# A decoder layer on one core: a tenth weight buffer in the space of the exponents, an earlier request for the fifth expert, a new timetable of the attention steps, and another order of loads and stores at the end

## The reference

```python
# 1. a mixer with cumulative sums over the tokens (cut)
out = (bil + alpha * tri) / counts + (bias_b + alpha * bias_t);  x += out @ Wo.T
# 2. cross attention, 16 heads of 32, 750 keys
x += softmax(Q @ K.T * SCALE) @ V @ Wo.T
# 3. experts that choose tokens: E = 32 experts, K = 8 tokens each, H = 2048
probs = softmax(x @ gate_w.T + gate_b, axis=tokens)
vals, idx = top_k(probs, K)                      # per batch and expert
merged = sum_k x[idx_k] * vals_k                 # one row per batch and expert
h = gelu([merged, 1] @ w1[e]);  o = [h, 1] @ w2[e]
x[idx_k] += o * vals_k                           # scattered back
```

## Time and profile before

| | us |
|---|---|
| median of 3 runs | 2212.28 |
| lowest and highest | 2208.69, 2214.53 |
| profiled execution | 2212.52 |
| its span in the profile | 2210.8 |

### The profile page before, as it was taken

One profiled execution on the slowest core, in us unless ns is written; L12 is line 12 of the kernel. 1 busy time (PEld: TensorE's weight loads), 2 busy tenths in 40 slices (PEclk: granted clock), 3 DMA queues, 4 the chain that ended last, 5 costly groups with the idle time before them and its releaser, 6 DMA issues. The chain is left out here.

```text
span 2210.8 us, 41404 instructions
## 1 busy us (share of the span) xinstructions
PE 1842.7 (83%) x12594; PEld 1207.2 (55%) x12594; DVE 1011.4 (46%) x2542; ACT 747.3 (34%) x1551; POOL 823.9 (37%) x591
## 2 busy tenths in 40 slices
PE   7889999999999999999999999986665656655644
PEld 5667777777777776777777767753111111111111
DVE  1355757657667676676676665751100000000003
ACT  3144435435454454454444544542100000000000
POOL 0255545555555556555555565552000000000000
PEclk9799999999999999999999999988877777777776
DMA  5324333243243333332433333266999999999996
GB/s 171 84 68 101 81 91 98 76 101 82 77 105 83 88 94 83 92 85 76 109 83 84 95 85 89 70 240 233 406 422 421 423 421 420 421 422 421 420 365 238
DMA packets 142370, 421.35 MB, mean 191 GB/s; under 512 B 32140, under 2 KB 78188, under 8 KB 117756
## 3 DMA queue, kind: packets, MB, share of 16 engines
q1 hardware_dynamic: 135580, 411.70, 54.6%
q10 hardware_dynamic: 5760, 8.15, 1.0%
q0 software_dynamic: 992, 1.02, 0.1%
HBM read 307.37 MB, written 17.14 MB: 147 GB/s over the span
## 5 line engine op out<-in xcount | busy, mean ns | idle before, releaser
L1172 DVE TENSOR_REDUCE maxes<-bank 112x1 f32<-112x376 f32 (+1 forms) x1024 | 511.3, 539 | 118.5 <-PE bank L1393 114.9
L974 ACT ACTIVATE probs<-bank 125x448 f32<-125x448 f32 x768 | 400.0, 547 | 140.5 <-PE bank L1415 139.5
L1809 PE MATMUL bank<-ring,hid_T 128*32 128x512 f32 x1024 | 177.9, 858 | 201.3 <-DMA ring<-in_L_ffn_w 196.4
L848 POOL TENSOR_TENSOR psum_keys<-psum_keys,probs 125x896 f32<-125x896 f32 x127 | 266.7, 2100 | 211.9 <-ACT probs L974 202.5
L1415 PE MATMUL bank<-q_st,k_st 98*125 98x224 f32 x1536 | 334.6, 304 | 8.5 <-DMA q_st<-max_two 5.6
L1393 PE MATMUL bank<-k_st,q_st 96*112 96x376 f32 (+1 forms) x1024 | 318.9, 357 | 21.3 <-DVE maxes L1172 18.1
L1415 PEld LDWEIGHTS bank<-q_st,k_st 98*125 98x125 f32 x1536 | 256.8, 190 | 61.3 <-issue 33.5
L1713 DVE TENSOR_TENSOR o_fin<-bank,b_row 16x512 f32<-16x512 f32 x32 | 21.7, 678 | 586.6 <-PE bank L1762 586.6
L851 POOL TENSOR_TENSOR psum_keys<-psum_keys,probs 125x896 f32<-125x896 f32 x127 | 266.8, 2100 | 10.0
L1642 POOL DMA_DIRECT2D o_rows<-o_fin x31 | 15.3, 492 | 595.4 <-DVE o_fin L1713 595.4
L1809 PEld LDWEIGHTS bank<-ring,hid_T 128*32 128x32 f32 x1024 | 44.9, 151 | 310.3 <-issue 304.8
(11 more groups left out here) (171 smaller groups left out, 2742.5 us busy)
## 6 DMA issues: line engine op xcount, KB each, us to landing
ring<-in_L_ffn_w SPq DMA_DIRECT2D x128, 2048.0 KB, 30.7
k_st<-k_hi SPq DMA_DIRECT2D x512, 93.8 KB, 2.1
k_st<-k_lo SPq DMA_DIRECT2D x256, 93.8 KB, 2.2
q_st<-q_hi SPq DMA_DIRECT2D x504, 28.0 KB, 1.8
ctx_nat<-in_ctx SPq DMA_DIRECT2D x16, 750.0 KB
x_in<-in_x SPq DMA_DIRECT2D x16, 448.0 KB, 3.9
out<-x SPq DMA_DIRECT2D x16, 448.0 KB, 3.1
out<-ring ACTq DMA_DIRECT2D x28, 256.0 KB, 3.1
```

What stands on the lines that cost most here:

```text
L848: nc.gpsimd.tensor_tensor(psum_keys[:], psum_keys[:], lo, ALU.add).then_inc(pool_chain, 1)
L974: nc.scalar.activation(probs[n % 2][:, j, :], bank[5 + u % 2][0:SK, 0:2 * T], ACT.Exp, scale=SCALE).then_inc(probs_ready, 1)
L1172: nc.vector.tensor_reduce(maxes[:, j, t, c:c + 1], score_bank(n)[0:TT, 0:SC[c + 1] - SC[c]], AX.X, ALU.max).then_inc(s_drained, 1)
L1809: last = nc.tensor.matmul(bank[5 + e2][c * 32:(c + 1) * 32, :], hid_T[:, e2, t, c * 32:(c + 1) * 32], ring[:, slot, col:col + D], start=(t ...
```

## The change

1. **Tables.** `TIMETABLE`, `AT` and `MAXIMA` get other entries. The last third of a group's values moves from step 1 to step 2, and the denominators are made right after them; POOL's sums stand at steps 6, 12 and 13 in place of 5, 11 and 14.
2. **A tenth buffer.** `probs` and `psum_keys` are placed in one stretch of memory that later is `tenth`. In the tail SP waits for the last denominators (`den_done`) and for slot 1, and asks for expert 2's second chunk into `tenth`, ahead of `recall_routed`. In the expert block the same stretch holds `o_in`, `picks` and a new `spread`, so POOL clears `picks` only after expert 2's first product (`h_full` 3), and SP loads `picks` after expert 3's weights.
3. **Expert 4.** Its two w1 chunks go into slots 0 and 1 as soon as expert 0 has used the first half (`first_half`) and the second (`h_full` 1).
4. **Rows.** `o_rows` is gone. POOL moves each expert's rows from `o_fin` into `o_in` directly, in four transfers (`place_rows`); DVE waits for the placing of the expert two before. The last expert's row is not moved: its bias is loaded ahead, and a product by `spread` (PE, `place_last`) puts the sum of its parts into place, which DVE adds, once per cycle.
5. **End.** All four chunks of the last expert are asked for before the loads of the output. Its w2 comes by steps (`load_steps`, 4 KB pieces), so that PE can start with one chunk. Stores of the 28 tiles are shared by ACT's queue (even) and SP's queue (odd).

```diff
@@ tables
-AT = {"keep": (1, 2), "mixer_stats": (0, 1), "mixer_root": (0, 2), "mixer_apply": (0, 3),
-      "bias": (0, 7), "attention_stats": (1, 4), "attention_root": (1, 4),
-      "attention_apply": (1, 5), "router_stats": (0, 12), "router_root": (1, 3),
-      "router_apply": (1, 12), "top": (2, 6), "exp": (2, 9), "weight": (2, 9),
+AT = {"keep": (1, 0), "mixer_stats": (0, 1), "mixer_root": (0, 1), "mixer_apply": (0, 2),
+      "bias": (0, 7), "attention_stats": (1, 4), "attention_root": (1, 5),
+      "attention_apply": (1, 6), "router_stats": (1, 1), "router_root": (1, 4),
+      "router_apply": (1, 13), "top": (2, 6), "exp": (2, 7), "weight": (2, 8),
       "scale": (2, 9)}
-LAST_PV_AT = 1
-SUM_AT = {5: 0, 11: 1, 14: 2}
+LAST_PV_AT = 2
+SUM_AT = {6: 0, 12: 1, 13: 2}
-MAXIMA = ((3, 3, 3, 1, 2, 2, 0, 0, 0, 1, 1),
-          (0, 1, 0, 0, 0, 3, 1, 3, 1, 2, 1, 2, 2),
-          (1, 2, 1, 0, 2, 2, 0, 2, 2, 0, 1, 1, 2),
-          (4, 0, 1, 0, 1, 2, 1, 1, 0, 2, 1, 2, 1))
+MAXIMA = ((2, 3, 3, 1, 2, 2, 0, 0, 0, 0, 2, 1),
+          (0, 0, 0, 0, 0, 3, 0, 4, 3, 0, 1, 2, 3),
+          (3, 1, 0, 0, 2, 2, 0, 0, 3, 1, 1, 2, 1),
+          (4, 0, 0, 2, 2, 0, 1, 0, 0, 3, 2, 0, 2))
@@ tail of the attention block, SP
                         first_weights([7])
+                        sp.wait_ge(den_done, 4 * B)
+                        sp.wait_ge(chunk_in[1], 16)
+                        load_chunk(sp, 2, 1, None, 1, tenth[:, 0:2 * H])
                         recall_routed()
@@ expert block, SP
                 weights(0, 0, True)
                 weights(0, 1, True)
+                for q in range(2):
+                    sp.wait_ge(first_half if q == 0 else h_full, 1)
+                    sp.wait_ge(chunk_in[q], 32)
+                    load_chunk(sp, 4, q, q)
+                weights(1, 0, False, (2, 3))
+                weights(1, 1, False)
                 sp.wait_ge(cleared, 2)
...
-                weights(1, 0, False, (1, 2, 3))
-                weights(1, 1, False)
-                with sp.Fori(2, E // 2 - 1) as i:
+                weights(2, 0, False, (2, 3))
+                weights(2, 1, False)
+                with sp.Fori(3, E // 2 - 1) as i:
...
-                weights(end, 1, False, (0, 1))
...
+                weights(end, 1, False)
                 for g in range(-(-NT // PER)):
...
-                weights(end, 1, False, (2, 3))
...
+                for n in range(1, NT, 2):
+                    store(sp, n)
@@ expert block, POOL
-                nc.gpsimd.memset(picks[:], 0.0).then_inc(cleared, 1)
...
+                pool.wait_ge(h_full, 3)
+                nc.gpsimd.memset(picks, 0.0).then_inc(cleared, 1)
+                nc.gpsimd.memset(spread, 0.0).then_inc(spread_cleared, 1)
+                for e in range(E - 1):
+                    pool.wait_ge(o_out, e + 1)
+                    place_rows(pool, e, o_placed[e % 2])
@@ expert block, PE, after the last expert's w2
-                sum_parts(E // 2 - 1, 1, False)
+                def place_last(g):
...
+                    nc.tensor.matmul(bank[g * CYCLE % 8][:], spread[:, g, :], o_sb[:, 1, :],
+                                     start=True, stop=True).then_inc(last_spread, 1)
```

More of the change, by code:

```diff
@@ L480, in build @@
         ring = sb(es, "ring", [P, SLOTS + 1, 2 * H])
+        graves = ExitStack()
+        sums = sb(graves, "sums", [P, 20 * T])
+        probs = [sums[0:SK, i * 8 * T:(i + 1) * 8 * T].rearrange("p (j n) -> p j n", j=4)
+                 for i in range(2)]
+        psum_keys = sums[0:SK, 16 * T:20 * T].rearrange("p (j n) -> p j n", j=4)
+        graves.close()
+        tenth = sb(es, "tenth", [P, 20 * T])
         lay = ExitStack()
@@ L1517, in build @@
         lay.close()
+        RW = 4
+        GB = B // RW
+        LEAD = [r * T % P for r in range(RW)]
+        PICKS = LEAD[1] + T + 64
+        o_in = tenth[:, 0:GB * D].rearrange("p (g d) -> p g d", g=GB)
+        picks = tenth[:, GB * D:GB * (D + PICKS)].rearrange("p (g n) -> p g n", g=GB)
+        spread = tenth[:, GB * (D + PICKS):GB * (D + PICKS + P)].rearrange("p (g m) -> p g m", g=GB)
         hid = sb(es, "hid", [P, 2, BANK])
@@ L1526, in build @@
         o_fin = sb(es, "o_fin", [B, 2, D])
-        RW = 4
-        GB = B // RW
-        o_in = sb(es, "o_in", [P, GB, D])
-        LEAD = [r * T % P for r in range(RW)]
-        picks = sb(es, "picks", [P, GB, LEAD[1] + T + 64])
         b1_flipped = sem("b1_flipped")
@@ L1553, in build @@
         fin_ready = sem("fin_ready")
-        fin_stored = sem("fin_stored")
+        fin_stored = [sem(f"fin_stored{i}") for i in range(2)]
         NT = B * T // P
@@ L1710, in row_out @@
                     dve.wait_ge(b2_loaded[e2], i * 16 + 16)
[L1711 to L1712 removed]
+                    if not (isinstance(i, int) and i == 0):
+                        dve.wait_ge(o_placed[e2], i * 16 * GB)
                     nc.vector.tensor_tensor(o_fin[:, e2, :], bank[7][0:B, :], b2_row[:, e2, :],
@@ L1775, in expert @@
                         slot = home_of(slot)
-                        if extra is not None and kd < 2:
-                            slot = extra
+                        held = ring[:, slot, :] if extra is None else extra[kd // 2]
                         for c in range(HC):
@@ L1781, in expert @@
                                                     tok[:, e2, kd, :],
-                                                    ring[:, slot, col:col + BANK],
+                                                    held[:, col:col + BANK],
                                                     start=(kd == 0), stop=(kd == KD - 1))
+                        if first and e2 == 0 and kd == 1:
+                            last.then_inc(first_half, 1)
                     last.then_inc(h_full, 1)
```

150 lines of the change are left out of this document (87 added, 63 removed).

## The result

| | before | after |
|---|---|---|
| median of the runs (lowest, highest), us | 2210.49 (2206.55, 2214.53) | 2177.19 (2173.99, 2177.50) |
| profiled execution, and its span | 2212.52, 2210.8 | 2177.29, 2175.5 |

The ratio is 0.9846 with a 95% interval of 0.9824 to 0.9868: 1.5% faster. The forecast was 2177. The parts of its sum hit less well than the sum, and most of this text is about that.

A forecast was written before the change was run, and what follows sets the result against it. PE was taken to bound the attention loop, DMA bytes the experts, with DMA engines idle near the end. From 2212.5 us, less 7 (prefetch), 24 (end) and 4 (table), came 2177.5, set at 2177; range 2156 to 2196.

The forecast's parts named there:

- 1, prefetch: Start of experts: weights requested earlier fill idle DMA time; 5.0 + 3.9 - 1.5 = 7.4, taken as 7 us faster.
- 2, end: Last expert's weights before output loads, no readbacks, loads and stores covering PE's work: 24 us faster (15 to 28).
- 2, placing of the rows: Expert stage: four POOL transfers of 8 KB per expert in place of one of 32 KB cost nothing.
- 3, table: Attention loop: new tables change PE's waits on DVE; sign unsettled, taken as -4 us (-22 to +14).
- The term of `picks`: Expert stage: 0.46 MB of picks move from idle DMA time into the full stage, costing 1 to 2 us.
- The cover for the late recall: Tail of attention: recall of the routed rows, queued five us later, still lands 4 us before its copy needs it.
- The slack of the chain: End: PE and DVE finish tiles near 2171 to 2175, under the DMA's 2184; more than 9 us late would decide.
- rival B: End bound by the chain, not bytes, with odd stores queued behind output loads: -14 in place of -24, 2187; chance 0.08.
- Rival D: Expert stage: placing transfers run one after another and the bias row holds SP's order: +72, about 2249; chance 0.02.
- neither wait looks shorter, the second may grow: Attention loop: PE's two waits on DVE per batch; the second may grow by one maximum, 0.5 us a batch, 7 us.
- rival A: Attention loop: the table decides more, removing most idle PE time (-20, 2161) or adding waits (+14, 2195); chance 0.20.
- near 2138 less what the table gives: Sign at the end: when the last chunk of weights lands, given as 2145 less 7, less the table's gain.

The follow-up runs named there:

- a_dram: The changed kernel, but POOL stores each expert's rows to DRAM in one 32 KB transfer and never brings them into o_in (output incomplete): 2164.29 us, ratio 0.979.
- a_noprefetch: The changed kernel without the tenth buffer's load in the tail and without the early request for expert 4's first matrix: 2185.32 us, ratio 0.9875.
- a_oldtab: The changed kernel with all the tables of before: 2189.59 us, ratio 0.9901.
- b_endorder: The changed kernel with the last expert's second matrix again behind the loads of the output: 2189.10 us, ratio 0.9896.
- d_maxold: The changed kernel with the old MAXIMA (score products per step) and all else of the new tables: 2196.77 us, ratio 0.9918.
- c_dram4: The changed kernel, but each expert's rows go in four transfers of four rows to DRAM, not into o_in (output incomplete): 2176.83 us, ratio 0.983.
- c_readback: The changed kernel with each expert's rows stored to DRAM in one 32 KB transfer and read back late in four 256 KB transfers over 128 partitions: 2169.09 us, ratio 0.9797.

## Why the prediction was right, and where it wasn't

| step | forecast | measured |
|---|---|---|
| 1, prefetch | -7 (4 to 9) | -6.1 (a_dram's middle piece, less `picks`), -8.3 (a_noprefetch, without `picks`) |
| 2, end | -24 (15 to 28) | -27.5 |
| 2, placing of the rows | 0 | +9.1 (a_dram's middle piece), +9.8 (its B) |
| 3, table | -4 (-22 to +14) | -10.7 (first piece), -12.1 (a_oldtab) |
| sum | -35 | -35.3 (spans); first numbers of the rows: -35.2 |

**Bound of the kernel.** Right: PE still waits for weights in each expert, and what the expert block costs goes by how fast the chunks are complete.

**Prefetch.** Right in mechanism, and nearly in size. By the gap alone the second chunk and expert 4 were to give 8.9 us, and a_noprefetch shows 8.3. The term of `picks` was too small: it had 1 to 2 us, the estimates from the trace are 2.5 and 4.5, and between the 8.4 us of a_noprefetch and the 6.1 of a_dram lie 2.3. So 6.1 is left where the sum had 7.4. The cover for the late recall held: PE waits 1.00 us for DVE's copy to `tok` as before (1.01), and the product starts 1.4 us after the transpose. The tenth chunk was asked for at 1503.61, which is 20.9 us ahead of expert 0's product; the last denominators of before stand 20.8 us ahead of it, so that this is as I had taken it.

**End.** Right in mechanism, 3.5 us too small. From the last half of w2 to the end it takes 36.8 us where my step had 41.5: by the time PE used the last weights, 1.4 MB of output had already been loaded, which my step let begin only then. After that loads and stores ran at 387 and 392 GB/s, near the 377 and 380 of the sum. From the start of the last half of w2 to the first tile it took 6.8 us (2138.66 to 2145.41) where the step has 5.5 (2145.5 to 2151) and its terms, 2.6 + 0.6 + 0.9 + 0.7, give 4.8; the first scatter products, 2 us from 2143.39, were not among them. The slack of the chain covered it. The order alone is worth 12 to 14 us (b_endorder), and rival B didn't come: stores go out on both queues from 2146 and 2148, and the share stays at 1.03.

**Placing.** Here the step failed that says "Nothing". It weighed POOL's time (0.56 us for one of 124 issues, free indeed) and the landing of expert 30's row (in time, indeed), and left out what these 124 transfers do to the others: with 8 KB each into SBUF beside a full queue the rate is 416 GB/s and not 421, the 16 KB packets take 633 ns in place of 620, and the engines drift apart, so that an expert takes 20.40 us in place of 20.06. It needs both edits of a_dram to get the time back: one transfer into SBUF has B +3.6, four to DRAM +0.0, one to DRAM -9.8. What exactly holds the engines up stays open. Rival D had the small transfers in view, but with a mechanism that didn't come (one after another, held by the bias row): no loop waits for them, the weights themselves come later. That a transfer of 8 KB beside 8 MB of weights could matter by its effect on the rest was not among my cases.

**Table.** The step that failed reads "neither wait looks shorter, the second may grow". It weighed the number of the maxima behind the statistics in the second quarter, 15 against 16, and not where they stand: the new row has 3, 4 and 3 at steps 5, 7 and 8, the old one 3, 1, 3 and 1 at steps 5 to 8 and more behind. That this is what shortened the waits is likely but not shown. The waits halved, 12.4 to 6.1 and 9.5 to 3.8 us, and PE's busy time in the window rose by 7.1 us, which is work pulled ahead. d_maxold shows that the four rows of counts together matter by 21 us; which of their entries took the waits away no run shows. The transposes of the merged rows show it batch by batch: 13 periods took 1145.2 us before (271.3 to 1416.5) and 1137.7 after (274.1 to 1411.8), -7.5 at a clock of 1.00. The last batch went from 80.0 to 75.1 and the tail from 37.3 to 36.2, of which an unknown part is the clock, and the loop starts 2.8 us later: -10.7. By the count of the prediction, (1486.9 - 274.1)/14, a batch takes 86.6 us in place of the 87.2 that I expected. The size is that of a mild rival A, whose condition, idle time of PE behind DVE that goes away, is what happened.

**The sum.** It was hit because the misses cancel. By the pieces: placing +9.1 and prefetch +0.9 on one side, table -6.7 and end -3.5 on the other. That the forecast met the median to 1 us is therefore no proof of its steps; with the true price of the placing alone it would have been 2186.

The last chunk "near 2138 less what the table gives" was used at 2138.66, with the table's 10.7 already taken off: that is 11 us late by the prediction's own test, and the sign by which the placing could be seen. a_dram has 2126.60.

## What to carry to other kernels

When the DMA queue is the bound, count what other transfers do to the rate of the big ones, not only their bytes and their issue time: here small results that aren't needed until the end were 7 us cheaper through DRAM, in one transfer for each expert and a late readback over all partitions, than placed row by row in SBUF. A rate of bytes isn't enough either: ask when a chunk is complete. A transfer that fills an idle stretch ahead of a full queue is worth about its bytes over the rate, and the last input that PE needs belongs in front of the loads that only the stores need. When the parts of a sum have wide bounds, test each part by its own piece of the trace; a total that fits proves none of them.

## What the runs showed of the hardware that I had not expected

- **A few small transfers slow the rest.** Into SBUF, 32 KB per expert beside 8 MB: 416 GB/s in four transfers, 413 in one, 418 with a quarter of the bytes. To DRAM, 421 in one and 420 in four. Other partitions left the rate where it was (416 and 415), and cost time (B +6.3 and +8.7). In the change the 16 KB packets take 13 ns more on the mean than in before, the 8 KB packets the same 317 ns; why is not shown by any run here.
- **Four-row transfers let the engines drift apart.** In c_dram4 the changeover between two sizes of packets takes 2.5 us at 1603 and 9.8 at 1993, with 16-row transfers to DRAM (a_dram) 2.2 and 2.8. An expert then takes 20.42 us in place of 20.06, and the 9 us that the higher rate should have won are gone.
- **Readback by shape.** 256 KB to 128 partitions keeps the DMA at 387 GB/s beside the output's loads (c_readback), where before's readbacks into 16 and 15 rows per block stood beside 171 and 175 GB/s. That those dips come from the shape is likely but was not tested by itself.
